# A pre-norm layer of linear attention and routed experts: attention rebuilt around shared products, LN2 rows made per slot tile

## The reference

```python
h = layernorm(x)                                   # x: (4, 512, 128)
q = elu(h @ wq + bq) + 1;  k = elu(h @ wk + bk) + 1;  v = h @ wv + bv
kv = einsum('bnhd,bnhe->bhde', k, v)
z = 1 / (einsum('bnhd,bhd->bnh', q, k.sum(axis=1)) + 1e-6)
x = x + einsum('bnhd,bhde,bnh->bnhe', q, kv, z).reshape(B, N, D) @ wo + bo
t = layernorm(x).reshape(2048, 128)
p = softmax(t @ Wr);  e = argmax(p);  p_max = max(p)
out = p_max * (gelu(t @ W1[e] + b1[e]) @ W2[e] + b2[e])      # W1: (8, 128, 512)
x = x + out
```

## Time and profile before

| | |
|---|---|
| median of 3 runs | 129.9 us |
| the profiled execution's time, its span | 130.67 us, 128.9 us |
| PE busy | 108.4 us (84%), 752 instructions |
| LDWEIGHTS busy (PEld) | 86.3 us (67%) |
| DVE, ACT, POOL busy | 65.2 us (51%), 53.2 us (41%), 61.5 us (48%) |
| 23 output scatters, mean | 971 ns each |
| 16 row scatters, mean | 1018 ns each |
| DMA moved | 13.78 MB |

### The profile page before, as it was taken

How to read it: one execution, slowest core, us unless ns; L and a number is a source line. 1 busy time by engine, 2 the same in 40 slices (tenths; PEclk the granted TensorE clock), 3 DMA queues, 4 the chain that set the end, 5 groups by cost and what they waited for, 6 DMA issues and landing times.

```text
span 128.9 us, 2594 instructions
## 1 busy us (share of the span) xinstructions
PE 108.4 (84%) x752; PEld 86.3 (67%) x758; DVE 65.2 (51%) x271; ACT 53.2 (41%) x168; POOL 61.5 (48%) x102
## 2 busy tenths in 40 slices
PE   5952979798999994999999739999999999999800
PEld 1330658676977851854644239999999999999700
DVE  3628927376587781185592301456446545544420
ACT  3042774376227001101400014766766776676400
POOL 3388580045081579780877100245544644644560
PEclk9999999999999999658999986999999999999997
DMA  3579999970000121130222179882110001001000
GB/s 95 176 122 353 392 304 288 353 213 2 0 0 0 44 88 41 45 120 0 81 89 105 66 205 244 246 245 75 41 41 33 16 29 41 13 30 41 0 0 0
DMA packets 13149, 13.78 MB, mean 107 GB/s; under 512 B 1568, under 2 KB 10688, under 8 KB 13136
## 3 DMA queue, kind: packets, MB, share of 16 engines
q1 hardware_dynamic: 11200, 10.24, 27.6%
q0 software_dynamic: 1504, 3.18, 7.2%
q10 hardware_dynamic: 432, 0.20, 0.5%
HBM read 9.37 MB, written 4.70 MB: 109 GB/s over the span
## 4 chain that ended last, share of the span: by engine, by line
PE 61%; DMA 9%; issue 8%; POOL 7%; DVE 6%; ACT 3%; SPq 2%; POOLq 1%; DVEq 0%
PE bank L882 17%; PE bank L893 15%; PE bank L741 5%; DMA bias_in<-in_L_attn_bo_dram 5%; POOL routed_rows L313 5%; PE bank L823 3%; PE bank L778 3%; PE bank L790 3%; PE bank L752 3%; PE bank L717 2%; PE bank L874 2%; DMA routed_rows<-rows,slot_at 2%; PE bank L728 2%; DMA slot<-routed_rows 2%; PE bank L742 1%
## 5 line engine op out<-in xcount | busy, mean ns | idle before, releaser
L320 POOL DMA_INDIRECT out_dram<-slot x23 | 22.3, 971 | 31.6 <-DVE slot L676 25.3
L439 ACT ACTIVATE hid<-bank,b_sb 128x128 f32<-128x128 f32 x92 | 26.3, 368 | 14.4 <-issue 10.7
L882 PE MATMUL bank<-tT,w_st 128*128 128x128 f32 x184 | 25.6, 284 | 0.0
L893 PE MATMUL bank<-w_sb,hid 128*128 x184 | 24.5, 276 | 0.6 <-issue 0.5
L823 PE MATMUL bank<-ones_bf 128*128 128x512 bf16 x85 | 22.9, 420 | 1.9 <-DVE ones_bf L454 1.5
L882 PEld LDWEIGHTS bank<-tT,w_st 128*128 128x128 f32 x184 | 23.7, 201 | 0.0
L893 PEld LDWEIGHTS bank<-w_sb,hid 128*128 128x128 f32 x184 | 22.4, 192 | 1.0 <-issue 1.0
L313 POOL DMA_INDIRECT routed_rows<-rows,slot_at x16 | 16.3, 1018 | 11.4 <-DVE slot_at L583 7.5
L671 DVE TENSOR_TENSOR yb<-bank,b_sb 128x128 f32<-128x128 f32 x23 | 6.7, 292 | 22.2 <-PE bank L893 17.8
L823 PEld LDWEIGHTS bank<-ones_bf 128*128 128x128 bf16 x88 | 9.1, 108 | 12.3 <-issue 4.1
L666 DVE COPY w_st<-w_sb 128x512 f32 x23 | 9.7, 426 | 9.2 <-PE bank L882 6.5
(11 more groups left out here) (121 smaller groups left out, 145.3 us busy)
## 6 DMA issues: line engine op xcount, KB each, us to landing
slot<-routed_rows SPq DMA_DIRECT2D x23, 130.0 KB, 2.8
w_sb<-in_L_ffn_W_dram SPq DMA_DIRECT2D x2, 1024.0 KB, 9.0
w_sb<-in_L_ffn_W_dram SPq DMA_DIRECT2D x4, 512.0 KB, 11.0
routed_rows<-pad_rows SPq DMA_DIRECT2D x1, 1040.0 KB, 8.9
x_sb<-in_L_attn_x_dram SPq DMA_DIRECT2D x4, 256.0 KB, 5.3
b_sb<-in_L_ffn_b_dram SPq DMA_DIRECT2D x1, 512.0 KB, 6.6
out_dram<-slot POOLq DMA_INDIRECT x23
routed_rows<-rows,slot_at POOLq DMA_INDIRECT x16
```

The costliest lines, as they stand in the source:

```text
L320: pool.indirect_dma_start(out=out_flat, out_offset=bass.IndirectOffsetOnAxis(ap=slot[:, i, D + NUMBER:D + NUMBER + 1].bitcast(U32), axis=0 ...
L439: act.activation(hid[:, i % 2, c, :], hid_ps[i % 2][:, c * P:(c + 1) * P], ACT.Gelu, bias=b1_sb[:, bass.ds(expert[i] * FC + c, 1)]).then_i ...
L882: last = pe.matmul(hid_ps[i % 2][:, c * P:(c + 1) * P], w1_st[:, i % W1_RING, c * P:(c + 1) * P], tT[:, i % RING, :], start=True, stop=True)
L893: last = pe.matmul(y_ps[i % 2][:, 0:D], hid[:, i % 2, c, :], w2_sb[c][:].rearrange("p e d -> p (e d)")[:, bass.ds(expert[i] * D, D)], star ...
```

## The change

**Router.** Wr, with its columns centred by a matmul (`centre`), stands beside wv (8 + 128 columns) and its product with wo beside wo, so the v product also gives x's part of the logits and the output product the attention's part (`x_logits`, `lg`). `rows_T`, `copy_hT` and `logits` are gone. The logits are found without LN2; only the exponent needs its scale (`scaled_logits`). **Rows.** A scattered row is the token, mean, scale, probability, number: 132 floats. POOL no longer makes normalised rows; DVE makes them per slot tile, after the fetch (`normal_rows`, a ring of 4). **Biases.** One host array of 144 columns with the four biases on partitions 0, 32, 64, 96; one bf16 matmul adds a bias to a whole batch, ahead of the fp32 ones, picked by `sel`. **Transfers.** wq, wk, Wr, wv, wo, bo are one host array, b1 is transposed on the host, x of batch 0 comes in two halves, and the bias comes first on ACT's queue. **PSUM** is one tensor with tiles that span bank ends; k has its own bank, shared with ks. **Order.** `product_o` of a batch stands one step later, after the next transposes; the fillers in the last steps are (2, 6, 4, 24), and the 4 after the first transposes are gone.

```diff
-            sp.dma_start(x_sb[:, tiles(0), :], x_v[0]).then_inc(x_in[0], 16)
-            sp.dma_start(x_sb[:, tiles(1), :], x_v[1]).then_inc(x_in[1], 16)
-            for i, bias in enumerate((bq, bk, bv, bo)):
-                sp.dma_start(bias_in[:, i * D:(i + 1) * D], bias.partition_broadcast(P)).then_inc(bias_in_s, 16)
-            for b in range(2, B):
+            for h in range(2):
+                hs = slice(h * J // 2, (h + 1) * J // 2)
+                sp.dma_start(x_sb[:, hs, :], x_v[0][:, hs, :]).then_inc(x0_in[h], 16)
+            for b in range(1, B):
                 sp.dma_start(x_sb[:, tiles(b), :], x_v[b]).then_inc(x_in[b], 16)
-            sp.dma_start(wo_sb[:], wo).then_inc(wo_in, 16)
-            sp.dma_start(wr_sb[:], Wr).then_inc(wr_in, 16)
...
+            def x_logits(b):
+                pool.wait_ge(v_s, b + 1)
+                pool.tensor_tensor(x_lg[:, tiles(b), :], v_sb[:, tiles(b), 0:E],
...
+                pool.wait_ge(xlg_ch, b + 1)
+                pool.tensor_tensor(x_lg[:, tiles(b), :], x_lg[:, tiles(b), :],
+                                   bo_logits[:].unsqueeze(1).broadcast_to([P, J, E]), ALU.add).then_inc(xlg_s, 1)
...
+                if b < B - 1:
+                    pool.wait_ge(mv2_s, J * (b + 1))
+                    pool.tensor_scalar(ve2[:, tiles(b)], rows[:, tiles(b), SCALE], LN_EPS, None, ALU.add)\
+                        .then_inc(ve2_s, 1)
+                pool.wait_ge(ve2_s, b + 1)
+                pool.tensor_tensor(rows[:, tiles(b), SCALE], ve2[:, tiles(b)], minus_half[:], ALU.pow).then_inc(rs2_s, 1)
...
             pool.wait_ge(number_s, 1)
+            x_logits(1)
             ln2(0)
+            x_logits(2)
+            scatter_rows(0, range(J))
             ln2(1)
-            scatter_rows(0)
+            x_logits(3)
+            scatter_rows(1, range(J))
             ln2(2)
-            scatter_rows(1)
+            scatter_rows(2, range(J - 1))
             ln2(3)
-            scatter_rows(2)
-            scatter_rows(3)
+            scatter_rows(2, range(J - 1, J))
+            scatter_rows(3, range(J))
...
+                act.wait_ge(lms_s, b + 1)
+                act.activation(ex[:, tiles(b), :], lms[:, tiles(b), :], ACT.Exp).then_inc(ex_s, 1)
...
+            normalise(0, range(J // 2, J))
+            act.wait_ge(wor_mm, 1)
+            act.copy(w_sb[:, WOR:WOR + E], wor_ps).then_inc(wor_s, 1)
+            act.copy(bo_logits[:], bo_ps).then_inc(bo_s, 1)
+            copy_xnT(0)
+            normalise(1, range(J // 2))
+            exp_q(0)
+            normalise(1, range(J // 2, J))
+            exp_k(0)
+            copy_v(0)
...
+                dve.wait_ge(bias_in_s, 16)
+                step(dve.tensor_scalar(bias_in[0:2 * QUAD, E:E + D], bias_in[0:2 * QUAD, E:E + D], 1.0, None, ALU.add))
+                step(dve.tensor_copy(bias_hi[:], bias_in[:]))
+                dve.wait_ge(step_s, 9)
                 step(dve.scalar_tensor_tensor(out=bias_rest[:], in0=bias_hi[:], scalar=part_step[:, 0:1],
-                                              in1=bias_b[:], op0=ALU.mult, op1=ALU.add))
+                                              in1=bias_in[:], op0=ALU.mult, op1=ALU.add))
                 step(dve.tensor_copy(bias_mid[:], bias_rest[:]))
                 dve.scalar_tensor_tensor(out=bias_rows[:], in0=bias_mid[:], scalar=part_step[:, 1:2],
                                          in1=bias_rest[:], op0=ALU.mult, op1=ALU.add).then_inc(bias_done, 1)
...
+                dve.wait_ge(xlg_s, b + 1)
+                dve.tensor_tensor(lg[:, tiles(b), :], att_ps[:, :, D:DE], x_lg[:, tiles(b), :], ALU.add)\
+                    .then_inc(lg_s, 1)
...
+            def scaled_logits(b):
+                ts = tiles(b)
+                dve.wait_ge(rs2_s, b + 1)
+                dve.wait_ge(lm_s, b + 1)
+                dve.tensor_tensor(lms[:, ts, :], lm[:, ts, :], rows[:, ts, SCALE:SCALE + 1].broadcast_to([P, J, E]),
+                                  ALU.mult).then_inc(lms_s, 1)
...
+            bias_parts()
             moments1(0)
             moments1(1)
-            dve.wait_ge(nmr1_s, 1)
-            for t in range(J - VEC, J):
-                dve.tensor_scalar(xn[:, t, :], x_sb[:, t, :], rs1[:, t:t + 1], nmr1[:, t:t + 1], ALU.mult, ALU.add)\
+            dve.wait_ge(rs1_s, 1)
+            for t in range(J // 2):
+                dve.tensor_scalar(xn[:, t, :], x_sb[:, t, :], mv1[:, t, 0:1], rs1[:, t:t + 1], ALU.subtract, ALU.mult)\
                     .then_inc(xnv_s, 1)
...
+            dve.wait_ge(w_in, 16)
+            dve.tensor_copy(bo_cols[:], w_sb[:, BO:BO + 1].broadcast_to([P, P])).then_inc(bo_cols_s, 1)
...
+            feature_k(0)
+            for s in range(1, B):
+                if s >= 2:
+                    residual(s - 2)
+                head_blocks(s - 1)
+                if s >= 2:
+                    moments2(s - 2)
                     route(s - 2)
-                if s == B:
-                    last_rows(B - 1)
-                    top_probability(B - 2)
-                    slots(B - 2)
+                attend(s - 1)
+                if s >= 2:
+                    scaled_logits(s - 2)
+                    slots(s - 2)
+                feature_k(s)
+                if s >= 2:
+                    top_probability(s - 2)
+                feature_q(s)
+            residual(B - 2)
+            head_blocks(B - 1)
+            moments2(B - 2)
+            attend(B - 1)
+            route(B - 2)
+            scaled_logits(B - 2)
+            slots(B - 2)
+            top_probability(B - 2)
+            residual(B - 1)
+            moments2(B - 1)
+            route(B - 1)
+            scaled_logits(B - 1)
+            slots(B - 1)
             top_probability(B - 1)
...
+            def normal_rows(i):
+                dve.wait_ge(slot_in[i], 16)
+                if i >= H_RING:
+                    dve.wait_ge(tT_mm, i - H_RING + 1)
+                dve.tensor_scalar(hb[:, i % H_RING, :], slot[:, i, xs], slot[:, i, MEAN:MEAN + 1],
+                                  slot[:, i, SCALE:SCALE + 1], ALU.subtract, ALU.mult).then_inc(h_s, 1)
...
             for i in range(W1_RING):
                 stage_w1(i)
             dve.wait_ge(b2_in, 16)
+            for i in range(3):
+                normal_rows(i)
...
                     stage_w1(i + W1_RING)
-                dve.wait_ge(slot_in[i], 16)
+                    normal_rows(i + 3)
                 output_rows(i)
...
+                pe.matmul(q_ps, bias_rows[:, E:E + D], sel[:, 0:1, :].broadcast_to([P, J, P]), start=True, stop=False)
+                pe.wait_ge(xnT_s, b + 1)
+                pe.matmul(q_ps, w_sb[:, WQ:WQ + D], xnT[:, tiles(b), :].rearrange("p j d -> p (j d)"),
+                          start=False, stop=True).then_inc(q_mm, 1)
...
+                pe.matmul(k_ps, sel[:, 1, :], bias_rows[:, E:E + D].unsqueeze(1).broadcast_to([P, J, D]),
+                          start=True, stop=False)
...
+                    last = pe.matmul(k_ps[:, j * D:(j + 1) * D], xnT[:, b * J + j, :], w_sb[:, WK:WK + D],
+                                     start=False, stop=j == J - 1)
+                last.then_inc(k_mm, 1)
...
+                pe.matmul(v_ps[:, 0:J - 1, :], sel[:, 2, :],
+                          bias_rows[:, 0:DE].unsqueeze(1).broadcast_to([P, J - 1, DE]), start=True, stop=False)
+                pe.matmul(v_ps[:, J - 1, :], sel[:, 2, :], bias_rows[:, 0:DE], start=True, stop=False)
+                for j in range(J):
+                    last = pe.matmul(v_ps[:, j, :], xnT[:, b * J + j, :], w_sb[:, WR:WR + DE], start=False,
+                                     stop=j >= J - 2)
+                last.then_inc(v_mm, 1)
...
+                pe.matmul(att_ps[:, 0, :], sel[:, 3, :], bias_rows[:, E:E + DE], start=True, stop=False)
+                pe.matmul(att_ps[:, 1:J, :], sel[:, 3, :],
+                          bias_rows[:, E:E + DE].unsqueeze(1).broadcast_to([P, J - 1, DE]), start=True, stop=False)
                 for j in range(J):
...
+                    last = pe.matmul(att_ps[:, j, :], scT[:, b * J + j, :], w_sb[:, WO:WO + DE], start=False,
+                                     stop=j in (0, J - 1))
...
+            def counts():
...
                 for a in range(B):
-                    last = pe.matmul(cnt_ps[:, CNT:CNT + E], ones16[:], total[:, a, :], start=a == 0, stop=a == B - 1)
+                    last = pe.matmul(cnt_ps, ones16[:], total[:, a, :], start=a == 0, stop=a == B - 1)
...
+            product_o(B - 2)
+            product_ks(B - 1)
+            keep_warm(WARM_LAST[0], warm2_ps)
+            product_nd(B - 1)
+            keep_warm(WARM_LAST[1], warm2_ps)
+            scores_T(B - 1)
+            rank_sums(B - 2)
+            keep_warm(WARM_LAST[2], warm2_ps)
+            product_o(B - 1)
+            keep_warm(WARM_LAST[3], warm2_ps)
+            counts()
             rank_sums(B - 1)
-            keep_warm(WARM_ROUTING)
```

(12 more changed lines are left out.)

600 lines of the change are left out of this document (265 added, 335 removed).

## The result

The changed kernel takes **118.9 us** (median of 4 runs, 118.2 to 121.17), the kernel before 130.17 (129.02 to 132.11) beside it. The ratio is 0.914, with a 95% interval of 0.902 to 0.926: faster by 8.6%. Ratios here leave out executions that are over 1.5% longer than the fastest of the same kernel, as 121.17 is. The forecast was 120.5 us, with a range of 117.0 to 124.5. The profiled execution took 118.2 us, with a span of 116.5 against 128.9.

The account below looks back on a forecast made before the run. It took a POOL queue fed by DVE to bound the middle, the path to the first ks product the beginning. Span 128.9 - 10.35 + 0.35 + 0.2 = 119.1, plus 1.77 gives 120.9; allowing for the median, 120.5 us, range 117 to 124.5.

Parts of the forecast that it names:

- First batch: Start of the kernel: with one narrow bias array first on ACT's queue, first ks product at 15.05, 1.9 us earlier.
- The batch cycle: Middle, from one batch's `sc` to the next: closes over DVE, listed terms 8.0 us plus about 0.5 for the v copy.
- the POOL loop: Middle: scatters, next scale, probability, next scatters set the time; last scatter starts at 60.15, 10.35 us earlier.
- almost without idle time: Sign to look for: POOL hardly idle between the first scatter and the scale of batch 3.
- The reason given for the middle: POOL sheds twelve row products of 0.45 us each; the larger part is scatters of batches 0 and 1 done earlier.
- Landing and fetch: After the last scatter: taken as before despite 528-byte rows instead of 1,040, with 0 and 1 us bounding the gain.
- The slot tiles: Last part: 1.89 us a tile kept; 0.35 us added for the first transpose, 0.2 for register values.
- the early rival: Shorter landing and fetch, earlier bias and no slow stretch at the slot tiles' start: 117.5 us; chance 0.15.
- The clock: Rival: clock halves in the last steps, around the last transposes, costing 2.9 us: 123.4; chance 0.22 together with a late start.
- It begins later: Rival at the start: bias or x lands 2 us late and holds DVE: 122.5; chance 0.22 together with the clock.
- POOL and DVE excluding each other in the slot tiles: Rival: a tile takes 2.62 us against 1.89, 16.8 us more in all, 137; chance of slower 0.03.

Follow-up runs that it names:

- the two runs with products: Changed kernel with eight extra row products on POOL, behind the scales of batches 1 and 2 or ahead of them: 123.0 us and 125.9 us.
- the one with POOL's order: Changed kernel with the scales of batches 1 and 2 ahead of the previous batch's fourth scatter, batch 3's logits product behind batch 1's scatters: 117.87 us.
- 15 fillers: Changed kernel with 15 instead of 24 fillers between the last output product and the last counts: 119.52 us.
- the control: The changed kernel itself run again, unedited, on the same chip as three variants: 119.19 us.
- wide rows: Changed kernel scattering and fetching rows of 1,040 bytes instead of 528, the added columns zeros: 120.34 us.
- one wait for the scale: Changed kernel with DVE's routing of a batch made to wait for POOL's second LN scale of that batch: 127.53 us.
- the eleven fillers put into holes: Changed kernel with six more fillers in the first batch and five behind TensorE's register loads, ahead of the first slot transpose: 118.30 us.

## Why the prediction was right, and where it was off

**First batch: right, 0.35 us late** (15.05 against 14.70). The bias landed 0.8 us sooner than taken (3.42 against 4.2); the five operations on it were put at 1.35 us, though their prices in the working add up to 1.48, and the moments began 1.48 us behind their start (4.90). The moments behind the bias operations, which the working put at 1.2 us of DVE's time, cost 0.65 on the path: undone, the first ks product came that much earlier.

**The batch cycle and the POOL loop: right in time.** Forecast and trace: `sc` of batch 0 19.85 and 19.58, of batch 1 28.6 and 27.9, first scatter 31.25 and 30.44 (16.20 and 15.74 behind the first ks product), scale of batch 2 46.5 and 45.8, last counts held by fillers to 54.0 and 53.34, last scatter 60.15 and 59.24. The cycle of a batch was taken as 8.75 us, where the listed terms add up to 8.5; it was 8.33. POOL was not "almost without idle time": it waited 1.07, 0.89, 1.93 and 1.73 us for others between its scatters. That the loop binds although POOL waits is what the two runs with products and the one with POOL's order show.

**The reason given for the middle was right and stopped one step short.** The prediction said that "the larger part is that the scatters of batches 0 and 1 are out of the way earlier". They are, by 10.29 and 10.13 us behind the first ks product. Why they can be earlier did not stand in it: the logits no longer pass over POOL's rows, so the routing begins 2.27 instead of 11.07 us behind its residual. The time came out right because the new order was followed step by step, not by luck. The row products named first, 5.2 us in all, are a small part: four of them, 1.75 us, stood on the way to the first scatter, which gained 10.29.

**Landing and fetch: 0.5 us too long.** Taken as before, 3.06 us from the last scatter to the first fetch; it was 2.53 (2.51 to 2.54 in eight variants, 2.71 and 2.72 with 15 fillers and in the control, 2.78 with wide rows). Why two kernels with short rows are at 2.7 is open. Bounds of 0 to 1 held it.

**The slot tiles: 0.8 us too long.** Their start was taken with the slow stretch of before; it ran at full clock in the profiled execution. The register load did not delay TensorE: it waited 1.45 us for rows. Small slips of the working changed nothing: 24 fillers from 49.0 end at 54.2, not 54.0; by the intervals of before the rows are there at 65.4, not 65.65; the early rival's terms give 117.1, not 117.5. So the span came out at 116.5 instead of 119.1: 0.91 at the last scatter, 0.53 in landing, 0.37 between first fetch and transpose, 0.79 in the tiles.

**The rivals.** The clock did not fall around the last transposes, where the prediction had looked (TensorE is at 1.00 there in the profiles of the changed kernel and of the control). It fell at the first slot tiles in the control and in the first batch in variants that do not touch it, which is the likely reason that the median lies 0.7 us above the profiled execution. The first batch is where the change took four fillers out, and there the prediction weighed no loss. The Trainium skill (TensorE: Matmul & The Clock Gate, Part 4) says that transposes do not count as work for the clock; what is seen agrees with it, a stretch with transposes and eight-column products in which the clock may fall and with fillers does not, but no run here tells transposes apart from mere lack of work. "It ends earlier" came true in part (fetch, bias and the slow stretch, together 1.7 us). "It begins later" was wrong in its cause, and its 1 to 2.6 us were seen through the clock. POOL and DVE excluding each other in the slot tiles did not come about: 1.89 us a tile with one and with two more DVE products. The exclusive lock that the Trainium skill (SBUF — State Buffer, SBUF: two separate sides) states is hardly put to the test by this: POOL's scatters start at 83.62 and 85.51 and take 0.97 us each, and DVE's W1 copy (84.64) and new product (84.97) fall between them.

## What to carry to other kernels

When work moves off a busy engine, look first at who was queued behind it and at what its result let start: here the routing began 8.8 us earlier, and one wait for the scale costs 8.65 us, while the products themselves took 0.45 each. A loop of small handoffs can bind although each of its engines idles, and a microsecond ahead of the handoff costs a whole one, behind it only what the wait does not cover. That one number comes back when one part is undone does not show that this part had made it: compare the points on the way. Before fillers are cut, see where the stretches are that they had carried; the eleven fillers put into holes here cost nothing that shows and took the scatter out of the times.
